# A graph kernel's edges by source: buckets filled to multiples of 128 instead of 256

## The reference

```python
edge_index = jnp.stack([src, dst])          # node = src, edge = dst
xh = (x @ W).reshape(N, 8, 32); eh = (hyperedge_attr @ W).reshape(M, 8, 32)
alpha = leaky_relu(sum(concat([xh[node], eh[edge]]) * att), 0.2)
alpha = softmax of alpha over the edges of a node
out_e = segment_sum(Binv[edge] * alpha * xh[node], edge)
out_n = segment_sum(Dinv[node] * alpha * out_e[edge], node)
x = layernorm(x + out_n)
```

```python
m = segment_sum(h[src], dst) * rsqrt(deg_in)        # h = x * rsqrt(deg_out)
y = m @ W_gc + b_gc + x @ W_res + b_res
y = batch_norm(y + moe(y))                          # 64 experts, the best two for each node
out = layernorm(x + y)
```

## Time and profile before

| | us |
|---|---|
| median of 3 runs (lowest to highest) | 6747.68 (6726.24 to 6759.04) |
| profiled execution | 6724.62 |
| its span | 6723.0 |
| PE / DVE / POOL / ACT busy | 4425.0 / 4409.4 / 3340.0 / 2123.9 |

### The profile page before, as it was taken

The page is one execution under the profiler, slowest core; times in us unless marked ns, Lnnn a source line. Parts: engine busy times, 40 slices in busy tenths (PEclk is TensorE's granted clock), DMA queues, the critical chain, the costliest instruction groups (busy, mean ns, idle before and its releaser), DMA issues. The chain is left out here.

```text
span 6723.0 us, 109009 instructions
## 1 busy us (share of the span) xinstructions
PE 4425.0 (66%) x22321; PEld 2740.4 (41%) x22368; DVE 4409.4 (66%) x9246; ACT 2123.9 (32%) x3871; POOL 3340.0 (50%) x3127
## 2 busy tenths in 40 slices
PE   6999988875333333366666665566666663999873
PEld 3455543332000000144444444444444342777751
DVE  8999988888999999766666665444444355111126
ACT  0000024445999999411211112100000000333222
POOL 1000027664555555477777774477777745111135
PEclk9999999998666666588888887777777766999985
DMA  0000026665000100155666656344444543888852
GB/s 6 17 9 10 9 52 148 145 147 128 30 27 27 31 27 27 41 99 97 97 96 96 96 96 93 126 155 148 152 153 151 210 112 122 272 274 271 264 169 80
DMA packets 367985, 724.35 MB, mean 108 GB/s; under 512 B 77240, under 2 KB 222142, under 8 KB 359712
## 3 DMA queue, kind: packets, MB, share of 16 engines
q0 software_dynamic: 144624, 351.35, 25.8%
q1 hardware_dynamic: 216080, 340.13, 15.4%
q10 hardware_dynamic: 7200, 32.03, 1.2%
HBM read 504.82 MB, written 187.10 MB: 103 GB/s over the span
## 5 line engine op out<-in xcount | busy, mean ns | idle before, releaser
L112 POOL DMA_INDIRECT slots_by_target<-pay,target_slot x831 | 948.4, 1141 | 669.3 <-PE OE L966 431.2
L1043 POOL DMA_INDIRECT rowsS<-hyperedge_rows,idxS x928 | 1013.2, 1092 | 340.4 <-issue 281.0
L1500 POOL DMA_INDIRECT rows<-h_table,idxT x880 | 914.3, 1039 | 394.8 <-issue 249.9
L1520 PE MATMUL pm<-rows,ohT 128*128 128x257 f32 x1760 | 679.9, 543 | 434.7 <-DVE big L1581 410.3
L966 PE MATMUL OE<-Pb,xs 128*32 128x512 f32 (+1 forms) x2352 | 410.9, 863 | 738.5 <-DVE xs L830 738.5
L1581 DVE TENSOR_TENSOR big<-big,pm 128x257 f32 x880 | 372.2, 423 | 713.7 <-issue 458.5
L1520 PEld LDWEIGHTS pm<-rows,ohT 128*128 128x128 f32 x1760 | 427.5, 266 | 664.1 <-issue 593.9
L1096 PE MATMUL pmS<-rowsS,ohS 128*128 128x256 f32 x1856 | 633.5, 501 | 86.8 <-DVE rowsS L1217 78.6
L448 PE MATMUL placed_sums<-onehot_tile,onehot_row 128*128 128x464 f16 x3328 | 670.8, 360 | 0.3 <-DVE onehot_tile L515 0.3
L656 PE MATMUL running<-onehot_edge,onehot_node 128*128 128x512 bf16 (+1 forms) x2738 | 542.1, 352 | 131.5 <-SPq L588 109.9
L811 DVE SCALAR_TENSOR_TENSOR Pb<-negative_b,ai,low 128x1251 f32<-128x1251 f32 x392 | 584.6, 1510 | 14.3 <-ACT low L897 14.3
(11 more groups left out here) (337 smaller groups left out, 7244.3 us busy)
## 6 DMA issues: line engine op xcount, KB each, us to landing
w<-in_L_gnn_w_dram SPq DMA_DIRECT2D x322, 512.0 KB
expert_inputs<-zeroE SPq DMA_DIRECT2D x64, 1024.0 KB
log_counts<-snap POOLq DMA_DIRECT2D x49, 625.5 KB, 5.2
negative_log_counts<-log_counts ACTq DMA_DIRECT2D x49, 625.5 KB, 3.3
negative_log_counts<-no_edge POOLq DMA_DIRECT2D x49, 625.5 KB
log_counts_in<-negative_log_counts SPq DMA_DIRECT2D x49, 625.5 KB, 3.8
xt<-expert_inputs SPq DMA_DIRECT2D x161, 128.0 KB, 2.8
expert_outputs<-ye POOLq DMA_DIRECT2D x161, 128.0 KB, 3.8
```

The source lines that it names most:

```text
L112: self.pool.indirect_dma_start(self.table[:, :], bass.IndirectOffsetOnAxis(ap=self.slot[:, c:c + 1], axis=0), self.pay[:, c, :], None, bou ...
L1043: pool.indirect_dma_start(rows[:, n % B, q, :], None, k.OEB[:, :], bass.IndirectOffsetOnAxis(ap=idx[:, n * Q + q:n * Q + q + 1], axis=0), ...
L1500: pool.indirect_dma_start(rows[:, n % B, q, 0:FEAT], None, k.H[:, :], bass.IndirectOffsetOnAxis(ap=idx[:, n * Q + q:n * Q + q + 1], axis=0 ...
L1520: pe.matmul(pm[:, q, 0:FEAT + 1], oh[:, u, q, :], rows[:, u, q, :], start=True, stop=True).then_inc(s_mm, 1)
```

## The change

The source order is filled to multiples of 128 like the target order. It has room for 880 tiles, and what was done for a pair is done for a tile: a table entry, SP's register read and go, the copy of the bucket's `u`, VectorE's register read and addition. The two constants for tiles become one (`NT`), the three tables rows of one tensor. In `phase_messages_back` TensorE writes the sums of two tiles into the two halves of one bank.

```diff
-PAIR = 2 * P
-
-NT = -(-2 * (EDGES // PAIR + NTILE) // 16) * 16
-NTM = 4 * P
-
-NTT = -(-(EDGES // P + NTILE) // 16) * 16
-NTTM = 7 * P
+
+NT = -(-(EDGES // P + NTILE) // 16) * 16
+TPP = 7
+NTM = TPP * P
...
-                unit = (PAIR, P)[j]
-                o(dve.tensor_scalar(tiles[:, :], pB[:, 0, 0:NTILE], float(unit - 1), None, ALU.add))
+                o(dve.tensor_scalar(tiles[:, :], pB[:, 0, 0:NTILE], float(P - 1), None, ALU.add))
                 o(dve.tensor_copy(tilesi[:, :], tiles[:, :]))
-                o(dve.tensor_scalar(tilesi[:, :], tilesi[:, :], (8, 7)[j], None, ALU.arith_shift_right))
+                o(dve.tensor_scalar(tilesi[:, :], tilesi[:, :], 7, None, ALU.arith_shift_right))
                 o(dve.tensor_copy(tiles[:, :], tilesi[:, :]))
-                o(dve.tensor_scalar(tiles[:, :], tiles[:, :], 1.0, float(unit // P), ALU.max, ALU.mult))
+                o(dve.tensor_scalar(tiles[:, :], tiles[:, :], 1.0, None, ALU.max))
...
+                o(dve.tensor_tensor(cmp[:, :, :], ends[:, :].unsqueeze(1).to_broadcast([P, TPP, NTILE]),
+                                    tnum[:, :].unsqueeze(2).to_broadcast([P, TPP, NTILE]), ALU.is_le))
+                o(dve.tensor_reduce(tabf[:, j, :], cmp[:, :, :], X, ALU.add))
+
+                o(dve.tensor_scalar(tabf[:, 2 - j, :], tabf[:, j, :], float(NTILE - 1), None, ALU.min))
...
             with sp.Fori(0, NT // Q) as i:
-                for q in range(Q // 2):
-                    bucket = sp.value_load(tab[0:1, bass.ds(i * (Q // 2) + q, 1)], min_val=0, max_val=NTILE)
+                for q in range(Q):
+                    bucket = sp.value_load(tab[0:1, bass.ds(i * Q + q, 1)], min_val=0, max_val=NTILE)
 
                     sp.wait_ge(s_evac, bucket + 1)
                     sp.sem_inc(s_go, 1)
...
                     pe.wait_ge(s_oh, n * (2 * Q) + 2 * q + 2)
-                    if q % 2 == 0:
-                        pe.wait_ge(s_go, n * (Q // 2) + q // 2 + 1)
+                    pe.wait_ge(s_go, n * Q + q + 1)
...
-        uq = sb("uq", [P, 2, Q // 2, 3, 2 * HEADS], BF16)
+        uq = sb("uq", [P, 2, Q, 3, 2 * HEADS], BF16)
...
-                    pool.wait_ge(s_mm, (n - B) * (Q // 2) + Q // 2)
+                    pool.wait_ge(s_mm, (n - B) * Q + Q)
...
-                pe.wait_ge(s_uq, n * (Q // 2) + Q // 2)
+                pe.wait_ge(s_uq, n * Q + Q)
...
-                                         uq[:, u % 2, q // 2, part, :], start=(part == 0), stop=(part == 2))
+                                         uq[:, u % 2, q, part, :], start=(part == 0), stop=(part == 2))
...
                 for q in range(Q):
-                    g = q // 2
                     if q % 2 == 0:
 
-                        pe.wait_ge(s_add, n * (Q // 2) + g + 1)
+                        pe.wait_ge(s_add, n * Q + q + 2)
                         pe.sem_inc(idle["pe"], 1)
-                    last = pe.matmul(pm[:, (u % 2) * (Q // 2) + g, 0:FEAT], oh[:, u % B, q, :], rows[:, u % B, q, 0:FEAT],
-                                     start=(q % 2 == 0), stop=(q % 2 == 1))
-                    if q % 2:
-                        last.then_inc(s_mm, 1)
+                    at = q % 2 * FEAT
+                    pe.matmul(pm[:, (u % 2) * (Q // 2) + q // 2, at:at + FEAT], oh[:, u % B, q, :], rows[:, u % B, q, 0:FEAT],
+                              start=True, stop=True).then_inc(s_mm, 1)
...
-                at = [act.value_load(tab[0:1, bass.ds(n * (Q // 2) + q, 1)], min_val=0, max_val=NTILE - 1) for q in range(Q // 2)]
+                at = [act.value_load(tab[0:1, bass.ds(n * Q + q, 1)], min_val=0, max_val=NTILE - 1) for q in range(Q)]
 
                 act.wait_ge(s_U, n + 1)
                 act.sem_inc(idle["act"], 1)
-                for q in range(Q // 2):
+                for q in range(Q):
...
-                return [dve.value_load(tab[0:1, bass.ds(n * (Q // 2) + g, 1)], min_val=0, max_val=NTILE - 1) for g in range(Q // 2)]
+                return [dve.value_load(tab[0:1, bass.ds(n * Q + q, 1)], min_val=0, max_val=NTILE - 1) for q in range(Q)]
 
             def add(n, u, at):
-                for g in range(Q // 2):
-                    m = k.big1[:, bass.ds(at[g], 1), :].rearrange("p a n -> p (a n)")
-
-                    dve.wait_ge(s_add, n * (Q // 2) + g + Q)
-                    dve.tensor_tensor(m, m, pm[:, (u % 2) * (Q // 2) + g, 0:FEAT], ALU.add).then_inc(s_add, 1)
+                for q in range(Q):
+                    m = k.big1[:, bass.ds(at[q], 1), :].rearrange("p a n -> p (a n)")
+
+                    dve.wait_ge(s_add, n * Q + q + 2 * Q)
+                    dve.tensor_tensor(m, m, pm[:, (u % 2) * (Q // 2) + q // 2, q % 2 * FEAT:q % 2 * FEAT + FEAT], ALU.add).then_inc(s_add, 1)
...
-        NI = NTT // Q
+        NI = NT // Q
```

More of the change, by code:

```diff
@@ L102, in on @@
     def on(self, pool):
-        self.pool, self.bound = pool, pool.to_reg(P * NTT - 1)
+        self.pool, self.bound = pool, pool.to_reg(P * NT - 1)
         return self
@@ L192, in _ @@
             sp.wait_ge(s_tabs, 1)
-            for j in range(2):
-                sp.dma_start(k.tab[j, :].rearrange("(p t) -> p t", p=P), tabi[0][:, j, :]).then_inc(s_out, 16)
-            sp.dma_start(k.tabD[0, :].rearrange("(p t) -> p t", p=P), tabi[1][:, :]).then_inc(s_out, 16)
+            for j in range(3):
+                sp.dma_start(k.tab[j, :].rearrange("(p t) -> p t", p=P), tabi[:, j, :]).then_inc(s_out, 16)
             sp.wait_ge(s_out, stored)
```

60 lines of the change are left out of this document (25 added, 35 removed).

## The result

The changed kernel takes 7131.67 us (median of 4 runs, 7124.23 to 7154.93) against 6751.88 us (4 runs, 6726.24 to 6759.04): ratio 1.0576, interval 1.0537 to 1.0614. It is slower by 380 us; the forecast was 7184 us, range 7085 to 7300. The profiled execution took 7154.93 us, its span is 7153.3.

What follows compares the result with a forecast made beforehand. The prediction took TensorE to bound placing, SP's go rate and TensorE nearly level in counting, and POOL's gathers messages back; -30 + 350 + 140 = +460 on 6724.6 us gave 7184 us, range 7085 to 7300.

Steps and rivals of the forecast that it cites:

- Placing: Projection and placing: matmuls 440 instead of 464 columns wide save TensorE time; -30 us, bounds -35 and -12.
- Counting: Counting stage: SP's look-up for each tile becomes the bound, 20.5 us a bucket against 13.1; +350 us.
- two delays for each copy are six, 4.1 us: Counting: each of a bucket's three 625 KB copies delays two of SP's loads, 4.1 us a bucket.
- Only undelayed loads: Counting: rival that a slower stage thins out the load delays, +155 us there; 6990 us in all, chance 0.07.
- Messages back: Messages back: four additions and four look-ups make VectorE's chain the bound, 6.6 us an iteration; +140 us.
- A: Prediction's theory in the follow-ups; for one more VectorE look-up in messages back: 0.71 us an iteration, stage +155 us.
- Faster: Counting and messages back: rival that look-ups are free; counting loses 41 us, messages 68; 6586 us, chance 0.03.
- only counting pays: Messages back: rival that VectorE's look-ups hide, -68 us there, the rest as forecast; 6977 us, chance 0.06.
- TensorE's clock: Counting: rival that TensorE drops to the 1.2 GHz level, 22.5 us a bucket, +450; 7284 us, chance 0.08.
- Every look-up costs 0.6 us: SP and VectorE: rival with that price per look-up, counting +415, messages back +403; 7513 us, chance 0.02.
- The conditions named beforehand: Counting and messages back: signs such as PE's go waits over 300 us, busy share near half, POOL waiting for sums.

Runs made afterwards that it cites:

- e12: Changed kernel with two of counting's three 625 KB copies per bucket cut to 2 columns, added copy's sign turned; 6990.39 us, counting 860.7 us.
- e6: Changed kernel with VectorE reading one unused table entry more per iteration of messages back, five instead of four; 7706.01 us, messages back 1640.7 us.
- e8: Changed kernel with two additions and two bare semaphore increments instead of four additions in messages back, four look-ups kept; 7482.70 us, messages back 1443.4 us.
- e5: Changed kernel unaltered, as the reference on a chip of the slower kind; 7505.22 us, messages back 1515.7 us.
- e10: Changed kernel with one read of four table entries on SP, ScalarE and VectorE; 6615.53 us, ratio 0.9816 to the kernel before.
- e7: Changed kernel with VectorE reading two table entries instead of four in messages back, four additions kept; 7434.43 us, messages back 1438.5 us.
- e1: Changed kernel with one read of four table entries on SP in counting instead of four reads; 7342.38 us, counting 902.7 us.
- e3: Changed kernel with POOL's 343 scatters moved from counting into softmax; 7573.17 us, counting 1006.8 us.

## Why the prediction was right

**The direction and the sum.** Three terms were forecast as -30, +350 and +140; they came to -33, +308 and +122. The sum of the three was 63 us too high. The profiled execution came out at 7154.93 us all the same, since the experts' stage was 29.5 us longer in it; against the median the forecast was 52 us too high. That is in part luck: by the medians the change costs 380 us where +460 was forecast, and a starting point 27 us under the median took a third of that error away.

**Placing: right.** TensorE's matmuls of that line went from 670.8 to 638.0 us, -33, between the -35 by columns and the -30 taken. VectorE did not stand in the way.

**Counting: the mechanism right, one term too large.** The undisturbed go (0.85 us mean over a pass) and the bucket's end (2.45, measured 2.46) were exact. The step that was off is "two delays for each copy are six, 4.1 us": there were 4.7, 3.08 us, and it is the third copy, the store (L708 before, L697 now), that gives one and not two. 2.46 + 16.43 x 0.85 + 3.08 = 19.5 us, which is what was measured. That the copies are the cause was inferred from their times; e12 showed it: without two of them 16.97 us, near the 16.4 that the prediction gave for no delays at all; one delay a bucket is left. "Only undelayed loads" had the right size for that case and the wrong condition: a slower stage doesn't thin the delays out.

**Messages back: right, 0.1 us an iteration high.** 2.90 us to L1204 (forecast 1.79 + 1.14), 3.00 to the one-hot (1.53 + 1.42), 0.61 to the next L1195 (forecast 0.69, the one-hot's whole length; the next instruction starts 0.08 us ahead of its end): 6.50 us, where 6.57 and 0.03 for the branch were forecast. e6 to e8 showed that reads and additions stand in one chain. An added read cost 0.56 us an iteration there and not 0.71, which is why A's +155 us were +125; the shared address and e5's own long iterations account for it.

**The rivals.** "Faster" and "only counting pays" fell: neither stage hid its look-ups. "Only undelayed loads" fell too, with 4.7 delays a bucket. e10 makes the condition of "faster" true in messages back; in counting it still costs 42 us where that rival had 41 us less. TensorE's clock fell, in counting from 0.95 to 0.87 and in messages back from 0.80 to 0.70, and bounded neither: SP had no pause between goes, VectorE none between iterations. "Every look-up costs 0.6 us" fell: SP's median is 268 ns and VectorE's 300. The floor of about 600 ns that the Trainium skill, "DMA: Bandwidth & Descriptors", latency and other measured facts, puts on a `tensor_load` is not seen in this case. What one look-up costs in all, 0.6 us on VectorE in e6, is near that figure, but half of it is register work behind the read.

**The conditions named beforehand.** Two signs were missed. PE's waits for goes were to pass 300 us and came to 246.2, and its busy share in counting was to be near a half and is 0.70: busy time per matmul of that stage is 698.6 / 2652 = 263 ns, where it was 199, so that it fills part of what was to show as waiting. A single matmul lasts 386 ns in the mean against 352 (377 against 379 in the median), so most of this is that tiles handed out one by one overlap less, and the smaller part the lower clock. The others came as written: 880 goes 1.04 us apart with no pause, POOL waiting for sums, four look-ups ahead of the one-hot.

## What to carry to other kernels

A table look-up on an engine's sequencer is work on that engine's path though the profile counts none of it as busy: price it by the distance of two look-ups in the trace, 0.6 to 0.8 us here, and set it against what one step of the stage takes. Here the finer granularity, which saves 5% of the tiles and doubles the look-ups, loses, and with one read for four entries it wins, so ask first whether the bookkeeping can be batched. Where an idle gap names a releaser that had long been done, look at the sequencer's own instructions in it, and settle it with one extra dummy look-up. If the sequencer's instructions don't fill it, look at when the semaphore changed: in e7 it was the signal that was late.

## What was not expected of the hardware

A read of four entries takes hardly longer than one: on SP 294 ns at the least against 261, on VectorE 343 against 300 in the median, 11 to 14 ns for each further register.

Bulk copies delay a sequencer's reads from their table, to 0.5 to 1.8 us, and with two of three copies cut to 2 columns, 1 of 4.7 delays a bucket is left (e12). On the chips of e1 to e8 SP also stops at semaphores, register instructions and branches, 3.5 to 9.4 times a bucket beside the delayed reads, and e3, with no such stop, shows that they need the scatters. On the same chips TensorE's signals in messages back come 0.64 to 1.80 us (medians) behind the matmul, where the others have 0.01. What in those chips makes the difference stays open.

POOL's gathers are held by some of VectorE's instructions. Two of the changed kernel's gathers in the iteration shown above, and one of the iteration ahead:

```profile
3708.59 1.01 POOL L1032 DMA_INDIRECT rowsS<-hyperedge_rows,idxS  x1 [2.13 <-PE pmS L1085]
3709.90 1.47 POOL L1032 DMA_INDIRECT rowsS<-hyperedge_rows,idxS  x1 [0.30 <-issue]
```

```profile
3702.81 1.01 POOL L1032 DMA_INDIRECT rowsS<-hyperedge_rows,idxS  x1 [0.30 <-issue]
```

The gather at 3709.90 started inside L1204 (3709.26 to 3710.48) and took 1.47 us; it ended 0.89 us after L1204 did. The one at 3708.59, during the additions, and the one at 3702.81, which began 0.14 us before its iteration's L1204, took 1.01. It is so throughout the stage: of 206 gathers that start inside an L1204 167 are lengthened and end 0.89 us behind it, and of 271 that start inside an addition none is. L1204 has two inputs in SBUF, the additions one in PSUM. The Trainium skill, "SBUF — State Buffer", in its section on SBUF's two separate sides, describes the port pair that VectorE and GpSimd share as an exclusive lock, which a VectorE instruction with two SBUF inputs takes against a GpSimd instruction that reads SBUF, and by that the trace agrees as to POOL. The other way round nothing is held here: the 171 L1204 that start inside a gather take 1.22 us like the rest. In the kernel after the longer gathers cost nothing visible, since POOL waits anyway.
